# An attention and expert layer on one core: residual, second norm, routing, sends, dt, B and C as single steps beside the slots

## What is computed

```python
h = _layernorm(x) * (1 + ca) + sa
proj = h @ W_in.T                      # gate 4096, hidden 4096, B 128, C 128, dt 64
h_BC = silu(conv(h_BC))                # four taps along the tokens
dt = jnp.clip(jax.nn.softplus(dt + dt_bias), 0.0)
At = A * dt
L_tri = jnp.exp(segsum(Ap))            # in chunks of 32 tokens
Yd = jnp.einsum('bclsh,bcshp->bclhp', Gm * L_tri, Hc)
yf = y * jax.nn.silu(gate)
yn = norm_w * (yf * jax.lax.rsqrt(var + EPS))
x = x + ga * (yn @ W_out.T)
h = _layernorm(x) * (1 + cb) + sb
probs = jax.nn.softmax(h @ gate_w.T)
topk_w, topk_idx = jax.lax.top_k(probs, K)
x = x + gb * (routed_out + silu(g) * u @ shared_down.T)
```

## Time and profile before

| | us |
|---|---|
| three runs | 1809.1, 1811.6, 1813.2 |
| median | 1811.6 |
| the profiled execution, its own time | 1820.6 |
| its span from first to last instruction | 1818.8 |
| PE busy | 1533.0 (84%) |
| DVE busy | 1349.9 (74%) |
| ACT busy | 922.5 (51%) |
| POOL busy | 703.2 (39%) |

### The profile page before, as it was taken

One profiled execution on the slowest core, in us unless ns is written; L12 is line 12 of the kernel. 1 busy time (PEld: TensorE's weight loads), 2 busy tenths in 40 slices (PEclk: granted clock), 3 DMA queues, 4 the chain that ended last, 5 costly groups with the idle time before them and its releaser, 6 DMA issues. The chain is left out here.

```text
span 1818.8 us, 33312 instructions
## 1 busy us (share of the span) xinstructions
PE 1533.0 (84%) x9484; PEld 1168.6 (64%) x9484; DVE 1349.9 (74%) x2124; ACT 922.5 (51%) x1696; POOL 703.2 (39%) x554
## 2 busy tenths in 40 slices
PE   6689999789998799997899997871739999999931
PEld 5466666566665566664666664851529999999920
DVE  3568887678887588886588885551478999998866
ACT  3465555465554655554655553310217877777710
POOL 0243443334342433432443440046745555445410
PEclk9699999899998999998999998575769999999965
DMA  4012221012221022220022210043448889888844
GB/s 146 0 36 69 61 61 52 0 52 61 69 61 35 0 63 67 61 68 18 17 61 66 64 55 3 1 141 117 156 147 276 287 285 290 281 283 271 253 168 157
DMA packets 111024, 198.12 MB, mean 109 GB/s; under 512 B 17481, under 2 KB 63063, under 8 KB 110816
## 3 DMA queue, kind: packets, MB, share of 16 engines
q1 hardware_dynamic: 98656, 171.75, 29.9%
q0 software_dynamic: 12288, 25.41, 3.8%
HBM read 160.96 MB, written 44.50 MB: 113 GB/s over the span
## 5 line engine op out<-in xcount | busy, mean ns | idle before, releaser
L1317 POOL TENSOR_TENSOR ssq<-ssq,ysq 128x512 f32<-128x512 f32 x128 | 164.3, 1284 | 466.8 <-ACT ysq L768 466.8
L973 DVE SCALAR_TENSOR_TENSOR e<-bank,scal,e 128x511 f32<-128x511 f32 (+2 forms) x384 | 287.4, 748 | 52.4 <-ACT e L763 17.1
L1363 POOL DMA_INDIRECT outputs<-hsw,x_rows x160 | 189.3, 1183 | 208.9 <-DVE hsw L1261 191.5
L396 PE MATMUL bank<-h_hi,wi_hi 128*128 x512 | 240.5, 470 | 19.0 <-POOL wi_lo L1304 14.6
L471 PE MATMUL bank<-e,wn 128*128 128x512 f32 x512 | 252.9, 617 | 0.0
L398 PE MATMUL bank<-h_hi,wi_lo 128*128 x512 | 204.6, 400 | 0.0
L397 PE MATMUL bank<-h_lo,wi_hi 128*128 x512 | 204.4, 399 | 0.0
L763 ACT ACTIVATE e<-bank,scal 128x512 f32<-128x512 f32 x128 | 99.7, 779 | 203.0 <-PE bank L398 203.0
L1304 POOL TENSOR_TENSOR wi_lo<-wi,wi_hi 128x512 fp32r<-128x512 f32 x128 | 165.2, 1291 | 51.0 <-ACT wi_hi L714 51.0
L885 DVE TENSOR_TENSOR ew_lo<-ew,ew_hi 128x864 fp32r<-128x864 f32 x160 | 169.3, 1058 | 20.6 <-ACT ew_hi L714 12.3
L714 ACT ACTIVATE ew_hi<-ew 128x864 fp32r<-128x864 f32 x160 | 145.6, 910 | 37.1 <-DMA ew<-expert_w 36.3
(11 more groups left out here) (244 smaller groups left out, 3622.3 us busy)
## 6 DMA issues: line engine op xcount, KB each, us to landing
ew<-expert_w SPq DMA_DIRECT2D x160, 432.0 KB
wi<-in_w SPq DMA_DIRECT2D x128, 256.0 KB, 2.7
x_rows<-grouped SPq DMA_DIRECT2D x160, 130.0 KB, 2.6
wo<-out_w SPq DMA_DIRECT2D x128, 128.0 KB, 2.4
got<-outputs SPq DMA_DIRECT2D x16, 768.0 KB, 4.3
grouped<-zeros_out SPq DMA_DIRECT2D x65, 130.0 KB
outputs<-hsw,x_rows POOLq DMA_INDIRECT x160
x_all<-x_t SPq DMA_DIRECT2D x4, 512.0 KB, 8.6
```

Of the source, the lines that this page charges most:

```text
L396: mm(out, w_hi, x_hi, start=first, stop=False)
L973: v.scalar_tensor_tensor(dst[:, d:], src[:, 0:SEQ - d], taps(TAPS - 1 - d), dst[:, d:], ALU.mult, ALU.add).then_inc(S[done], 1)
L1317: g_.tensor_tensor(ssq[:, :], ssq[:, :], ysq[:, :], ALU.add).then_inc(S["ssq_done"], 1)
L1363: g_.indirect_dma_start(outputs, bass.IndirectOffsetOnAxis(x_rows[:, i % XD, EMB:EMB + 1].bitcast(U32), 0), y_rows[:, i % YD, :], None, bo ...
```

## The change

The stages 1, 4 and 5 are taken apart into single steps, and each step is given a slot number. After slot j of batch b each engine runs `beside(b, j)`, which holds the steps due there:

- of batch b - 1: 1/rms, the scaling and the sum into x (slots 0 to 4), the second norm (6 to 15), logits to rows (16 to 24), the 24 sends (25 to 32, three a slot);
- of batch b + 1: dt, B and C (from slot 4; in batch 0 from slot 10);
- in batch 0 the first norm of batches 1, 2 and 3 (from slots 0, 9 and 18).

Routing works on four tiles (256 columns) at a time, with the counts so far carried in `base`; the rank of a batch comes from matmuls with `ones_r` instead of the sums over 16 tiles. The shares of batch b - 2 are worked out in slots 0 and 1. Only norm 0, dt, B and C of batch 0 stand ahead of the slots. The attention loops are written out instead of `Fori`. After the last batch `beside(4, j)` runs for j = 0 to 26, with the twelve shared units between its steps (`SHARED_AT`).

Some work changes engine: both low parts of h and the sum into x go from DVE to POOL; the gate's scaling of the output product (`gather_out`) and the six copies of h for the sends go to ACT; the second half of the zero fills is issued by ACT. The shared weights are loaded only after the last slot. The expert stage is the same.

```diff
+TAIL = {"std": 0, "inv": 1, "mm": 2, "scale": 2, "add": 4}
+NORM = {"mean": 0, "centre": 0, "square": 2, "variance": 3, "eps": 3, "std": 4, "rstd": 5, "spread": 6, "xhat": 6, "h": 7,
+        "low": 8}
+ROUTE = {"logits": 16, "lsub": 17, "exp": 18, "prob": 19, "top": 20, "taken": 21, "rank": 22, "key": 23, "rows": 24,
+         "turn": (21, 24), "copy": (22, 25), "send": 25}
+DTBC = {"dt": 0, "z": 0, "zabs": 1, "exp": 2, "ln": 3, "plus": 4, "turn": 5, "at": 5, "at_hi": 6, "at_lo": 7,
+        "bc": (8, 13), "tap0": (9, 13), "taps": (10, 14), "silu": 17}
+NORM_OF_NEXT = 9
+NORM_AT, DTBC_AT, DTBC_AT_FIRST = 6, 4, 10
+SENDS = 3
+GAP = 27
+SHARED_AT = (4, 6, 7, 8, 9, 10, 11, 13, 14, 18, 20, 22)
...
+            for e in range(0, EXPERTS // 2, 4):
...
+            def square_sums(c):
+
+                pe.wait_ge(S["ssq_done"], START["ssq_done"] + (c + 1) * PAIRS)
+                pe.wait_ge(S["rank_read"], 2 * c)
...
+                if j == TAIL["mm"]:
+                    pe.wait_ge(S["ssq_wide"], c + 1)
+                    pe.wait_ge(S["ssq_var"], c + 1)
...
+                seg_unit(b, 0, 0)
+                if b:
+                    square_sums(b - 1)
+                    pe.wait_ge(S["ssq_var"], b)
+                    pe.wait_ge(S["attn_scaled"], b * KE)
...
+            def gather_out(c):
+
+                act.wait_ge(S["out_mm"], START["out_mm"] + (c + 1) * PAIRS)
...
+                if b + 1 < BATCH:
+                    dve.wait_ge(S["normed_lo"], (BATCH + b) * KE)
+                    moving(b + 1, 0, 0)
+                    moving(b + 1, 0, 1)
...
+                if j >= ROUTE["send"]:
+                    n = SENDS * (j - ROUTE["send"])
+                    for s in range(n, min(n + SENDS, TILES * TOP_K)):
+                        send(c, s // TOP_K, s % TOP_K)
```

More of the change, by code:

```diff
@@ new lines, in program @@
+        mov_hi = sb("mov_hi", [P, 2, SEG_UNIT], F32R)
+        mov_lo = sb("mov_lo", [P, 2, SEG_UNIT], F32R)
+        xsq = h
+        zexp = zln = zabs
+        dt_head = z
+        acc_rows = xc[:, 0, :].rearrange("p (a n) -> p a n", a=2)
+        var, std, rstd = (sb(n, [P, TILES]) for n in ("var", "std", "rstd"))
+        attn = sb("attn", [P, KE, SEQ])
+        rinv_diag = rdiag
+        ms, rms, rinv = (sb(n, [P, TILES]) for n in ("ms", "rms", "rinv"))
+        prob = sb("prob", [P, TILES, EXPERTS])
@@ new lines, in program @@
+        rest = sb("rest", [P, TILES, EXPERTS])
+        key = sb("key", [P, TILES, EXPERTS])
+        lexp = pos = same_key = lsub
+        kept = shares = rest
+        before_r = sb("before_r", [P, P], F32R)
+        lmax, lsum, lrec, ksum, krec = (sb(n, [P, TILES]) for n in ("lmax", "lsum", "lrec", "ksum", "krec"))
+        top8 = sb("top8", [P, TILES, 8])
+        key8 = sb("key8", [P, TILES, 8])
+        base = sb("base", [P, EXPERTS])
+        rows6 = sb("rows6", [P, GTILES, TOP_K], U32)
@@ new lines, in mean @@
+            def mean(r):
+                b = r % BATCH
+                if r >= BATCH:
+                    pe.wait_ge(S["attn_res"], (b + 1) * KE)
+                    pe.wait_ge(S["attn_normed"], (b + 1) * KE)
+                elif r:
+                    pe.wait_ge(S["x_in"], 16 * BATCH)
+                    pe.wait_ge(S["xhat"], r * KE)
+                else:
+                    pe.wait_ge(S["first_in"], 32)
+                for k in range(KE):
+                    i = mm(p_norm[:, :], ones, x_all[:, k, tokens(b)], start=k == 0, stop=k == KE - 1)
+                i.then_inc(S["mean"], 1)
@@ L534, in _ @@
                 i.then_inc(S["g_mm"], 1)
+                beside(b, 0)
                 slot(b, 1, 1, do_out="")
+                beside(b, 1)
                 pe.wait_ge(S["g_done"], 2 * (b + 1))
-                slot(b, 2, 0, do_out="first")
-                slot(b, 3, 1)
-                with pe.Fori(2, PAIRS // 2) as jj:
-                    slot(b, 2 * jj, 0)
-                    slot(b, 2 * jj + 1, 1)
+                for j in range(2, PAIRS):
+                    slot(b, j, j % 2, do_out="first" if j == 2 else "mid")
+                    beside(b, j)
@@ L892, in _ @@
+            dve.wait_ge(S["first_in"], 32)
+            for k in range(KE):
+                centre(0, k)
             dve.wait_ge(S["setup"], SETUP)
@@ new lines, in _ @@
+            add_eps(0)
+            widen(0)
+            for k in range(KE):
+                scale(0, k)
+            dt_z(0)
+            dt_abs(0)
+            dt_plus(0)
+            dt_rows(0)
+            at_low(0)
+            moving(0, 0, 0)
+            moving(0, 0, 1)
+            for n in range(2):
+                for d in range(1, TAPS):
+                    bc_tap(0, n, d)
+            for b in range(BATCH):
+                if b:
+                    mean_square(b - 1)
+                for t in range(TILES):
@@ L1360, in scatter @@
+            for j in range(ROUTE["send"]):
+                beside(BATCH, j)
+            for s in range(TILES * TOP_K):
+                send(BATCH - 1, s // TOP_K, s % TOP_K)
             def scatter(i):
```

1269 lines of the change are left out of this document (685 added, 584 removed).

## The result

| | before | after |
|---|---|---|
| median of the runs, us | 1811.4 (1809.1 to 1813.2) | 1738.3 (1734.8 to 1740.2) |
| ratio | 1 | 0.960 (0.959 to 0.962) |
| the profiled execution, its own time | 1820.6 | 1739.2 |
| its span | 1818.8 | 1737.0 |

The change takes 73 us off, 4.0%. The forecast was 1724 with a range of 1674 to 1780.

The account below looks back on a forecast made before the run. PE sets the pace in the slots; around them stand serial stretches, sends and experts. Gains of 25 (head), 65 (between batches) and 106 (end), less 108 (slots), give 88 us less: 1732.6 profiled, 1724 median, range 1674 to 1780.

Parts of the forecast that it names:

- The end: Last output product to first x_rows load: 135 us instead of 241.7, a gain of 106 us (bounds 85 and 125).
- rival 3: After attention, PE stays at 1.2 GHz between interrupted shared units and fills are hindered more: 1780 us; chance 8%.
- The head: Before batch 0's segments: first mov_hi at 47 us instead of 72, a gain of 25 us (bounds 20 and 29).
- the variance starts behind that product: In the head: norm 0's variance follows the modulation product, at 21.3 us, not the means at 26.25.
- Between batches: Last output product to the next batch's segments: third unit 21.7 us earlier, three times, 65 us gained (bounds 58 and 68).
- started warm it takes 3.3: PE's first segment unit after each batch gap: 3.3 us instead of 5.2 at the lower clock.
- The slots: Steps added beside the attention slots cost 108 us: PE 58.5, DVE 36, ACT, POOL and segments 14 (bounds 65 and 150).
- Elsewhere it pays what exceeds 0.48: In slots without added PE steps, DVE pays for work beyond its 0.48 us idle, less 0.4 lent between slots.
- rival 4: In the slots, only PE's own steps lengthen them and all else is hidden: 1674 us; chance 13%.
- Rival 1: In send slots, DVE's two-SBUF-input operations hold up POOL's sends: 46 us more, slots of 8 us, 1770 total; chance 12%.
- Rival 2: Sends in the slots starve other engines, a 36 us stall in each of three batches: 1832 us, slower; chance 5%.
- carry the difference over to the median: Final conversion: the sum uses before's profiled execution, 1820.6 against median 1811.6; the same difference turns 1732.6 into 1724.

Follow-up runs that it names:

- the head's experiment: On the combined-edits version that took 1686.7 us: ACT waits for the conditioning vector before anything else, DVE makes batch 0's h_lo; 1705.8 us, ratio 0.936 to before.
- the late units: Against the changed kernel: six of twelve shared units moved behind the rows, ACT's fills in groups of four ahead of them; 1733.3 us, ratio 0.952 to before.

## Why the prediction was right, and where its terms were off

**Removed waits (right in kind).** PE's waits between the batches, the second norm and the sends went as said. *The end* was the best term: 131.8 against 135, with rows at 85.9 (90) and 45.9 from rows to x_rows (45). Its size on the fills rested on two queues, and the fills on SP alone show that the second is worth 25 us. The 45 is partly luck: the forecast had six fills of a queue held up for 19 us, and in after's profile no group of four took more than 5.2; x_rows came 10 us behind the last fill instead. On chips on which groups were held it took 57 to 59. A unit took 4.2 (4.3 said), PE kept the higher clock in them (0.98 granted from 1152.7 to 1199), and rival 3 fell.

**The head: 17.7, not 25.** The step that failed is "the variance starts behind that product, at 21.3 (19.99 now, plus 1.3)". I put only the load of x ahead of the product and left out ACT, where the square and two table loads stood ahead of `cact`: 26.0. With the silu first 3.0 came back. The chain behind it was too short as well: from the variance to `mov_hi` the forecast has 25.7 us (21.3 to 47), and it took 28.2 (26.02 to 54.19), 1.6 of the difference in the variance itself, 3.56 us instead of 1.95 before. In the head's experiment it took 28.1 again (18.78 to 46.85). That `mov_hi` stood at 46.9 there is luck: the product ended 2.5 us earlier than forecast, and the chain was 2.4 longer.

**Between batches: 49.2 net, not 65.** Two mis-sizings. First, the step "started warm it takes 3.3". In batch 1 PE started 3.2 us behind the last product (2.6 forecast), but its first unit then took 4.85, to 325.48, with a matmul every 0.43 us and a granted clock of 0.61 until 324.7. The square sums and the second unit took 0.7 more than said. So the third unit started at 330.72, 13.3 behind the last product and not 10.5 (326.6), and from last product to first output product batch 1 gained 18.3, not 21.7. Second, batches 2 and 3 wait 5.7 and 5.8, not 3: the prediction moved the sends past POOL's square sums in the slots but not past the `mov_lo` behind the last slot. Putting three sends behind it gave 3.3 in both.

**The slots: 97.5, not 108**, from errors of both signs.
- PE's own steps took 60.9 us (matmuls of added lines, start to start; which step one counts a hand-over to moves this by 1); 58.5 was forecast.
- "Elsewhere it pays what exceeds 0.48": DVE 16, ACT 4, sends 5 and the port lock 5, 30 in all. Measured some 7, what the 97.5 leave beside PE's steps and the shares; about half of it is the sends', 1.2 in each of three batches. DVE's room is larger than the waits of the earlier trace rows show. PE's transposing step of 1.24 itself cost only 0.89, and 22 operations of DVE, spread out, cost 2.6 us in batch 2. Here rival 4, which has nothing, was nearer than the forecast.
- The shares, 19.8 forecast, took 29: 13.0 up to the first output product in each of two batches, and 1.7 and 1.5 in the slot behind it. 9.9 was their length. On top came products held by POOL (1.50 and 1.52 instead of 0.42, twice a batch) and PE's restart at the lower clock (a matmul of 512 columns every 0.43 instead of 0.23 us).

**Rival 1** (sends locked out) had its mechanism and not its price: 0.29 on one send of three, none on the others, and up to 0.98 on one send in each of the last two slots; slots of 6.48, not 8. **Rival 2** (starvation): no wait of this kind stands in the slots.

**From profile to median: 7.7 of the 14 us miss.** The sum gave 1732.6 for the profiled execution, which took 1739.2. I then took off 9 us because before's profile lay that far above its median; after's lies 0.9 above its own. The step "carry the difference over to the median" assumed that this excess belongs to code that the change keeps. It is not settled where it lay; what varied most here, by 10 to 22 us between chips, was the sends beside the fills, and the change cut 96 sends of that stretch to 24.

## What to carry to other kernels

Moving steps beside a busy loop costs what they take on the engine that sets the pace; on the others single short operations were nearly free here (0.12 us for one of 0.42), and the same operations in one block cost more than their length. Before moving a step, walk through each engine's order at the new place, setup code and the first transfers behind the loop included: the square ahead of the silu on ACT (3 us), three sends ahead of `mov_lo` (5) and the owners' chain behind the late units were all visible in the order of instructions. When one wait goes, look for the next in the thing that the waiter reads, not in what took its time before. And compare stretches that vary between chips only on one chip: against after's first profile, the late units seemed to give back 13 us that were the chip's.

## What was not expected of the hardware

- DVE operations with both inputs in SBUF stand still while POOL's tensor operations run, and don't get in between two of them: `y` takes 0.69 us alone and, in the median of its 20 cases beside `wi_lo`, 1.23, a share's product 0.42 alone and 5.65 beside three POOL operations in a row. The taps, `yt` and `xt` read one input from PSUM and keep 0.75, 0.74 and 0.69 in all cases. The Trainium skill (SBUF — State Buffer, two separate sides) says that whichever of the two starts first has the port pair for its whole instruction. The shares' row at 633.24 agrees: `wi_lo` had started at 633.20. The row of 5.65 goes further: by its record it had started 0.37 us ahead of the first of the three tensor operations, beside a send, and was held by all of them. By the broader reading of that rule, which rival 1 took, a send would be held as fully; here a send took 1.25 instead of 0.96 beside `m` in the slots, and 1.94 at most, beside `mov_hi`.
- A fill costs a queue 0.9 to 1.2 us; of 3.5 for four, 1.9 is the reading of their addresses from SBUF. Two queues brought the DMA engines to a share of 1.02 and 273 GB/s where no group was held up; one left them at 0.42 to 0.44.
- The same fills beside sends took 34 us for 32 a queue on one chip and 53 on another, with single groups of four standing for 20 us. What holds them was not tried.
